# Two attention blocks: projections to queries and keys from parts, and a new order of work at both ends

## Time and profile before

| | us |
|---|---|
| three runs | 1654.03, 1655.61, 1656.54 |
| the profiled execution | 1653.08 |
| its span, first to last instruction | 1651.3 |
| head, until the first score of block 0 | 47.4 |
| round 0, round 1 | 80.9, 93.4 |
| a steady round | 97.0 |
| last round with scores (round 15) | 84.0 |
| from the last score of block 0 to the end | 83.5 |

### The profile page before, as it was taken

One profiled execution on the slowest core, in us unless ns is written; L12 is line 12 of the kernel. 1 busy time (PEld: TensorE's weight loads), 2 busy tenths in 40 slices (PEclk: granted clock), 3 DMA queues, 4 the chain that ended last, 5 costly groups with the idle time before them and its releaser, 6 DMA issues.

```text
span 1651.3 us, 25703 instructions
## 1 busy us (share of the span) xinstructions
PE 1598.8 (97%) x9399; PEld 1071.2 (65%) x9399; DVE 1159.9 (70%) x1961; ACT 1068.6 (65%) x1826; POOL 1120.6 (68%) x531
## 2 busy tenths in 40 slices
PE   7898999999999999999999999999999999999988
PEld 5333566666676766667676676766666666676667
DVE  6676676777767777776777777677777767766342
ACT  1454666766676666667666676766667676666744
POOL 2487767876766777676687767678676667868700
PEclk8899999999999999999999999999999999999999
DMA  7404032040412314141130414114041411400000
GB/s 208 122 20 121 20 97 52 33 126 29 128 39 81 68 33 116 39 129 39 68 80 33 116 39 128 34 58 96 21 128 39 124 31 39 109 20 8 7 7 20
DMA packets 47660, 111.69 MB, mean 68 GB/s; under 512 B 5808, under 2 KB 6448, under 8 KB 47536
## 3 DMA queue, kind: packets, MB, share of 16 engines
q1 hardware_dynamic: 47248, 109.86, 23.8%
q10 hardware_dynamic: 288, 0.20, 0.0%
HBM read 67.84 MB, written 41.94 MB: 66 GB/s over the span
## 4 chain that ended last, share of the span: by engine, by line
PE 89%; DVE 5%; ACT 3%; DMA 2%; issue 1%; SPq 0%; POOL 0%; ACTq 0%; POOLq 0%
PE bank L938 14%; PE acc L863 14%; PE scores L906 14%; PE scores L845 14%; PE scores L893 7%; PE bank L947 4%; PE scores L885 3%; PE acc L943 3%; DVE halfmax L724 3%; PE scores L886 3%; PE scores L887 3%; PE bank L943 3%; PE bank L969 2%; PE bank L965 2%; ACT turned L579 1%
## 5 line engine op out<-in xcount | busy, mean ns | idle before, releaser
L518 POOL TENSOR_TENSOR sum<-sum,probs 128x1024 f32<-128x1024 f32 x444 | 1040.1, 2373 | 372.1 <-PE acc L863 372.1
L724 DVE TENSOR_REDUCE halfmax<-bank 128x1 f32<-128x512 f32 x1007 | 666.8, 685 | 232.6 <-PE bank L938 228.9
L559 ACT ACTIVATE probs<-scores 128x512 f32<-128x512 f32 x896 | 515.9, 598 | 186.8 <-PE scores L845 183.2
L845 PE MATMUL scores<-q_stack,k_stack 97*128 97x512 f32 x1024 | 447.9, 454 | 2.4 <-DMA q_stack<-neg 2.3
L938 PE MATMUL bank<-k_stack,q_stack 96*128 96x512 f32 x992 | 422.7, 444 | 19.1 <-DVE halfmax L724 8.6
L938 PEld LDWEIGHTS bank<-k_stack,q_stack 96*128 96x128 f32 x992 | 187.0, 191 | 139.9 <-DVE halfmax L724 75.4
L906 PEld LDWEIGHTS scores<-v,turned 128*128 128x128 f32 x1952 | 252.3, 191 | 38.7 <-ACT turned L579 19.2
L906 PE MATMUL scores<-v,turned 128*128 128x128 f32 x1952 | 259.5, 276 | 4.3 <-ACT turned L579 3.8
L845 PEld LDWEIGHTS scores<-q_stack,k_stack 97*128 97x128 f32 x1024 | 194.2, 191 | 98.0 <-issue 79.6
L572 ACT ACTIVATE probs<-scores,negmax 128x1024 f32<-128x1024 f32 x128 | 142.6, 1114 | 157.9 <-DVE negmax L763 157.9
L863 PE MATMUL acc<-probs,v 128*32 128x512 f32 x1792 | 221.9, 607 | 0.0
(11 more groups left out here) (102 smaller groups left out, 1376.4 us busy)
## 6 DMA issues: line engine op xcount, KB each, us to landing
q_stack<-parts_dram SPq DMA_DIRECT2D x96, 256.0 KB, 5.2
k_stack<-parts_dram SPq DMA_DIRECT2D x96, 256.0 KB, 7.0
xin<-x_dram SPq DMA_DIRECT2D x16, 512.0 KB, 3.5
parts_dram<-q_hi SPq DMA_DIRECT2D x16, 512.0 KB, 2.6
parts_dram<-q_lo SPq DMA_DIRECT2D x16, 512.0 KB, 3.1
parts_dram<-k_hi SPq DMA_DIRECT2D x16, 512.0 KB, 3.7
parts_dram<-k_lo SPq DMA_DIRECT2D x16, 512.0 KB, 4.1
x<-x_dram SPq DMA_DIRECT2D x16, 512.0 KB, 3.5
```

What stands on the lines that cost most here:

```text
L518: pool.tensor_tensor(total, total, probs[:, ring_slot(i, half, kt), 2 * two:2 * two + 2, :], ALU.add).then_inc(added[two], 1)
L559: act.activation(dst, score_bank(i, index), ACT.Exp).then_inc(exp_done, 1)
L724: dve.tensor_reduce(halfmax[:, h, t, half:half + 1], banks[p][:, :], AX.X, ALU.max).then_inc(bank_free[p][VE], 1)
L845: pe.matmul(score_bank(i, index), ks[0:SPLIT + 1, i % 2, h, tile(kt)], qs[0:SPLIT + 1, q_half(i, half), h, :], start=True, stop=True).then ...
```

## The change

It does five things.

1. `q` and `k` of block 0 (images 1 to 15) and of block 1 (images 0 to 14) are projected in three fp32r products instead of one in fp32. The weights are split once at the start, the normalized image in each round: `hi0`/`hi1` on ScalarE write `xh_hi` by the same instruction as `norm`, `lo0`/`lo1` on VectorE subtract.
2. The tables are dealt anew: places of the maxima, `norm0`, `save`, `affine`, `scale`, `form` and `rstd`; `exp1` of even tiles one gap later.
3. The head: statistics of image 1 before the first maxima, from x1, where the image is loaded third; values at gaps 18 and 19; `q` and `k` in another order.
4. In round 0 and the last round with scores the first value product stands alone at gap 5 (`pv_a`); before, it was the first of the pair at gap 11.
5. The last two rounds have tables of their own (ROUND_END, new LAST_AT and chain).

```diff
 def tile_pieces(t, first):
-            ("exp1", t, 0, None, first + 1, None),
-            ("rinv", t, 0, None, None, first + 3),
+            ("exp1", t, 0, None, first + 2 - t % 2, None),
+            ("rinv", t, 0, None, None, first + 3 + 2 * (t % 2)),
...
 NEXT0 = [
-    ("affine0", 0, 2, None, None, 61), ("norm0", 0, 2, None, GAPS + 1, None),
+    ("affine0", 0, 2, None, None, 59),
+    ("norm0", 0, 2, None, GAPS + 0, None),
+    ("hi0", 0, 2, None, GAPS + 0, None),
+    ("lo0", 0, 2, None, None, GAPS + 3),
...
-    ("norm1", 0, 0, None, GAPS + 31, None), ("q1", 0, 0, GAPS + 36, GAPS + 36, GAPS + 37),
+    ("norm1", 0, 0, None, GAPS + 32, None),
+    ("hi1", 0, 0, None, GAPS + 32, None),
+    ("lo1", 0, 0, None, None, GAPS + 35),
+    ("q1", 0, 0, GAPS + 36, GAPS + 36, GAPS + 37),
...
 HEAD = [
-    ("norm0", 0, 0, None, 4, None),
-    ("q0", 0, 0, 5, 5, 6), ("q0", 1, 0, 5, 5, 6), ("k0", 0, 0, 7, 7, 8), ("k0", 1, 0, 7, 7, 8),
-    ("v0", 0, 0, 9, 9, None), ("v0", 1, 0, 9, 9, None),
+    ("norm0", 0, 0, None, 0, None), ("stats0", 0, 1, None, None, 0),
+    ("q0", 0, 0, 1, 1, 1), ("k0", 0, 0, 2, 2, 2), ("mean0", 0, 1, 3, None, 3), ("k0", 1, 0, 4, 4, 4),
+    ("q0", 1, 0, 5, 5, 5), ("var0", 0, 1, 6, None, 6),
 ] + [("max", n, 0, 10 + n, None, 10 + n) for n in range(FIRST)] + [
-    ("stats0", 0, 1, None, None, 20), ("mean0", 0, 1, 24, None, 24), ("var0", 0, 1, 28, None, 28),
-    ("affine0", 0, 1, None, None, 10 + FIRST),
+    ("v0", 0, 0, 18, 18, None), ("v0", 1, 0, 19, 19, None), ("affine0", 0, 1, None, None, 20),
...
-FIRST_MAX = [g for g in (*range(4), *range(10, 22)) for _ in range(2)]
+FIRST_MAX = [*range(4), *(g for g in range(10, 24) for _ in range(2))]
...
+    ("pv_a", 0, 0, 5, None, None), ("pv_b", 0, 0, 11, None, None)] + [
...
+def end_tile_pieces(t, offset, first):
+    return [("score1", (t, 0), offset, first, None, None), ("score1", (t, 1), offset, first + 1, None, None),
+            ("max1", t, offset, None, None, first + 1), ("exp1", t, offset, None, first + 1, None),
+            ("rinv", t, offset, None, None, first + 3), ("turn", t, offset, first + 4, first + 4, None),
+            ("pv1a", t, offset, first + 7, first + 7, None), ("pv1b", t, offset, first + 7, None, None)]
...
-LAST_AT = {tile: LAST_FIRST + LAST_SPACE * n for n, tile in enumerate(LAST_TILES)}
+LAST_AT = {tile: LAST_FIRST + LAST_SPACE * n + 3 * (tile[1] == -1) for n, tile in enumerate(LAST_TILES)}
...
+LAST_CHAIN = [
+    ("save", 1, -1, None, 4, None), ("sums", 1, -1, 4, 4, None), ("recip", (1, 0), -1, None, None, 5),
+    ("recip", (1, 1), -1, None, None, 5), ("recip", (1, 2), -1, None, None, 8), ("recip", (1, 3), -1, None, None, 8),
+    ("proj", 1, -1, 14, None, 14), ("stats1", 1, -1, None, None, 14),
+    ("mean1", 0, -1, 16, None, 15), ("var1", 0, -1, 17, None, 16), ("affine1", 0, -1, None, None, 17),
+    ("norm1", 0, -1, None, 18, None),
+    ("q1", 0, -1, 20, 20, 20), ("q1", 1, -1, 20, 20, 20), ("k1", 0, -1, 22, 22, 22), ("k1", 1, -1, 22, 22, 22),
...
+ROUND_LAST = LATER + [p for p in folded(VALUES) if p[2] == -1] + LAST_CHAIN + LAST_BLOCK1 + [
...
+NOT_IN_ACC = (("k0", 0, 0), ("q0", 0, 1), ("k0", 0, 1))
...
 @block.sync
             sp.dma_start(wts[:, :, :], weights).then_inc(const_loaded, 16)
+            sp.dma_start(x1[:, 1, :], x_dram[1]).then_inc(x1_loaded, 16)
...
-            for i in range(3):
+            load_shift(0, 0)
+            for i in (0, 2):
                 sp.dma_start(x1[:, i, :], x_dram[i]).then_inc(x1_loaded, 16)
-            load_shift(0, 0)
...
 @block.scalar
+            def high_norm(b, i):
+                before = parts_user_before(b, i)
+                if before:
+                    act.wait_ge(bank_full[bank_of(before)], filled(before))
+                act.wait_ge(affine_done[b], i + 1)
+                src = xin[:, :] if b == 0 else x1[:, i % 3, :]
+                act.activation(xh_hi[:, :], src, ACT.Identity, bias=gn[b][:, OFFSET:OFFSET + 1],
+                               scale=gn[b][:, GAIN:GAIN + 1]).then_inc(xh_high_done[b], 1)
...
+            act.wait_ge(prep_ve, 4)
+            for n in range(4):
+                act.copy(w_hi[:, n, :], weight_of(n)).then_inc(w_high_done, 1)
...
 @block.vector
+            def low_norm(b, i):
...
+                dve.wait_ge(norm_done[b], i + 1)
+                dve.wait_ge(xh_high_done[b], parts_before(b, i) + 1)
+                dve.tensor_tensor(xh_lo[:, :], xh[:, :], xh_hi[:, :].bitcast(F32),
+                                  ALU.subtract).then_inc(xh_low_done[b], 1)
...
+            for n in range(4):
+                dve.wait_ge(w_high_done, n + 1)
+                dve.tensor_tensor(w_lo[:, n, :], weight_of(n), w_hi[:, n, :].bitcast(F32),
+                                  ALU.subtract).then_inc(w_low_done, 1)
...
 @block.tensor
-                    pe.wait_ge(norm_done[b], i + 1)
-                    weight = wq_scaled[:, b, :] if name[0] == "q" else w(b, WK)
-                    mm = pe.matmul(dst[:, :], weight, xh[:, halves(arg)], start=True, stop=True)
+                    n = 2 * b + (name[0] == "k")
+                    if in_parts(b, i):
+                        pe.wait_ge(w_low_done, 4)
+                        pe.wait_ge(xh_low_done[b], parts_before(b, i) + 1)
+                        pe.matmul(dst[:, :], w_hi[:, n, :], xh_hi[:, halves(arg)], start=True, stop=False)
+                        pe.matmul(dst[:, :], w_hi[:, n, :], xh_lo[:, halves(arg)], start=False, stop=False)
+                        mm = pe.matmul(dst[:, :], w_lo[:, n, :], xh_hi[:, halves(arg)], start=False, stop=True)
+                    else:
+                        pe.wait_ge(norm_done[b], i + 1)
+                        mm = pe.matmul(dst[:, :], weight_of(n), xh[:, halves(arg)], start=True, stop=True)
```

More of the change, by code:

```diff
@@ L94 @@
 ]
 CHAIN = [
[L96 to L100, removed]
@@ new lines @@
+    ("sums", 0, 0, 45, 45, None),
+    ("recip", (0, 0), 0, None, None, 51),
+    ("recip", (0, 1), 0, None, None, 52),
+    ("recip", (0, 2), 0, None, None, 54),
+    ("recip", (0, 3), 0, None, None, 57),
+    ("proj", 0, 0, 60, None, 62),
+    ("stats1", 0, 0, None, None, 62),
+    ("save", 1, 0, None, GAPS + 3, None),
+    ("sums", 1, 0, GAPS + 7, GAPS + 7, None),
+    ("recip", (1, 0), 0, None, None, GAPS + 10),
+    ("recip", (1, 1), 0, None, None, GAPS + 11),
+    ("recip", (1, 2), 0, None, None, GAPS + 14),
@@ new lines @@
+END_AT = {(n % KT, n // KT - 2): TILE_FIRST + TILE_GAPS * n - GAPS for n in range(3, 3 + KT)}
+TILE_PIECES = ("score1", "max1", "exp1", "rinv", "turn", "pv1a", "pv1b")
+END_PIECES = [("out", 0, -2, 16, None, 16), ("pv_a", 0, 0, 5, None, None), ("pv_b", 0, 0, 11, None, None),
+              ("affine1", 0, -1, None, None, 30), ("norm1", 0, -1, None, 33, None)]
+ROUND_END = [p for p in ROUND if p[0] not in TILE_PIECES and p[:3] != ("pv", 0, 0)
+             and p[:3] not in [q[:3] for q in END_PIECES]] + END_PIECES
@@ L133 @@
+END_TILES = folded([p for (t, offset), first in END_AT.items() for p in end_tile_pieces(t, offset, first)])
 DIRECT = 2
@@ L181, in pieces_of @@
 def pieces_of(kind, i, engine, gap, images):
-    table = HEAD if kind == "head" else ROUND_FIRST if i == 0 else ROUND_LAST if i == images else ROUND
+    table = (HEAD if kind == "head" else ROUND_FIRST if i == 0 else ROUND_END if i == images - 1
+             else ROUND_LAST if i == images else ROUND)
     return [(p[0], p[1], i + p[2]) for p in table if p[engine] == gap and 0 <= i + p[2] < images]
@@ L212, in bank_uses @@
         if piece[0] in BANKED:
-            shared = (0, 1, 3, 4) if head_maximum(piece) else (0, 1)
-            b = 2 if piece[0] in IN_ACC and piece[1] == 0 else min(shared, key=lambda n: free[n])
+            shared = (0, 1, 3, 4) if in_head(piece) else (0, 1)
+            in_acc = piece[0] in IN_ACC and piece[1] == 0 and piece not in NOT_IN_ACC
+            b = 2 if in_acc else min(shared, key=lambda n: free[n])
             uses[piece] = (b, sum(counts[b]), counts[b][0], counts[b][1], last[b])
@@ L281, in bass_two_attention_blocks @@
         xh = sb("xh", [C, N])
+        xh_hi, xh_lo = (sb(n, [C, N], F32R) for n in ("xh_hi", "xh_lo"))
+        w_hi, w_lo = (sb(n, [C, 4, C], F32R) for n in ("w_hi", "w_lo"))
         part = [sb(n, [C, N], F32R) for n in ("q_hi", "q_lo", "k_hi", "k_lo")]
@@ L397, in turned_of, with hi_count, in_parts, parts_before @@
             return probs[:, 0, 2:4, :].rearrange("p h n -> p (h n)") if tile_set(j, t) else turned[:, :]
+        def hi_count(b, which, half, i):
+            order = ((0, 0), (1, 0), (1, 1), (0, 1)) if (b, i) == (0, 0) else ((0, 0), (0, 1), (1, 0), (1, 1))
+            return 4 * i + order.index((which, half)) + 1
+        def in_parts(b, i):
+            return i > 0 if b == 0 else i < images - 1
+        def parts_before(b, i):
+            return i - 1 if b == 0 else i
+        def parts_user_before(b, i):
+            if b == 0:
```

(6 more changed lines are left out.)

111 lines of the change are left out of this document (69 added, 42 removed).

## The result

The changed kernel takes 1761.29 us (median of 4 runs, 1760.03 to 1768.33) against 1655.63: a ratio of 1.0652, 95% interval [1.0635, 1.0669]. I had forecast 1632 us, faster.

What follows compares the result with a forecast made beforehand. TensorE, busy 97% of the span, was taken to bound the steady rounds. Terms of -17.3 - 1 + 4 - 4.5 - 1 - 4 = -23.8 us gave 1632 us; range 1616 to 1648 us, 8 times in 10.

Steps and rivals of the forecast that it cites:

- The shared reads of VectorE and GpSimd: At gaps 0 to 9: the two-SBUF-input subtraction might wait 0 to 2.35 us for GpSimd's addition, on average 1.2, twice a round.
- 4 us for all stalls that the parts bring: Steady rounds: splitting the image delays maxima and projections by 0.3 us a round over 14 rounds, +4 us.
- a rival of 0.07: Slower case, chance 0.07: each of 30 subtractions waits 1.2 us for GpSimd's addition and TensorE with it, 36 us; 1668 us.
- the rival's sign: Profile after: subtraction durations spreading up to 3.6 us beside GpSimd's additions would show the slower case at work.
- The projections: Queries and keys: three fp32r matmuls, 0.70 us, for one fp32 of 0.86; 108 in TensorE-bound rounds save 17.3 us.
- ScalarE's second pass: Writing xh_hi: one more ScalarE pass of 1.24 us per image and block, hidden in throughput by idle time.
- New places of the maxima: Steady rounds: 64 maxima dealt anew, within the 0.3 us a round charged for stalls; lower bound a gain of 1 us.
- The head: Before the first score: earlier first maximum 1.5, statistics moved 3.7, value projections costing 0.7; 4.5 us sooner, bounds 2 and 6.
- Rounds 0 and 1: GpSimd's first addition starts some 11 us sooner; 1 us gained in round 0, none in round 1; bounds +3 and -5 us.
- Tail and round 15: Last round before the tail and tail: copies 1 us, reordered work 2.5, last round 0.5; 4 us gained, bounds 0 and 8.
- The sum: Whole kernel: -17.3 - 1 + 4 - 4.5 - 1 - 4 = -23.8 us, forecast 1632 us, chance 0.51.

Runs made afterwards that it cites:

- e3: Changed kernel, with GpSimd made to wait before the addition that runs beside each subtraction until xh_lo is written; 1637.0 us, 0.9904 of the kernel before.
- e2: Changed kernel, with two bn_stats of one SBUF input on VectorE in place of each subtraction, xh_lo left zero; 1632.1 us, 0.9869 of the kernel before.
- e5: Kernel before, plus one unread VectorE subtraction with two SBUF inputs at gap 28 of every round; 1700.3 us in one run.
- e6: Kernel before, plus one unread VectorE subtraction in each of rounds 1 to 15, at gap 22 + i in round i; 1705.2 us in one run.
- e11: Kernel before, plus one unread VectorE subtraction in each of rounds 1 to 14, at gap 34 + 2i in round i; 1701.3 us in one run.
- e1: Changed kernel, with all query and key projections back to one fp32 matmul and no passes writing xh_hi and xh_lo; 1651.2 us, 0.998 of the kernel before.
- e7: Changed kernel with GpSimd's additions held for the subtraction, and image 0's values projected last in the head; 1630.6 us, 0.9849 of the kernel before.

## Why the prediction was wrong

The step that failed is "The shared reads of VectorE and GpSimd". I put the subtraction at 1.25 us into the sum, with 4 us for all stalls that the parts bring, and left the exclusion to a rival of 0.07. Where I had those 4 us, the exclusion alone measured 124 us (the changed kernel less e3) to 129 us (less e2). The mechanism of the rival is what happened, and I had it mis-sized twice. Its wait was to be what is left of one addition, 1.2 us on average; it was 3.5 us (4744 less 1226 ns), since 29 of 29 stood to the end of the row, and all 29 took longer than the 3.6 us that I had named as the rival's sign. And a stopped TensorE was to cost the stop alone; it cost the slow clock behind it too. For each of the 26 subtractions of the steady rounds that is 2.8 us of stop and 1.5 us of slow clock (72 and 39 us), where the rival had 1.2. So 1668 us became 1761. Against the case I had written that the wait "must reach TensorE through the maxima, under a pair of value products": for block 0 it did reach it, because behind the pair (553.80 to 555.7) only two maxima's matmuls, a score and `turn` were left before the next maximum needed a bank; for block 1 the projection one gap later had no cover that held, and TensorE waited for `xh_lo` itself. The rows that should have moved me were at hand: additions without a gap at both places where the subtraction was put. For block 0's place that is the earlier trace rows; for block 1's, about 761 us in that round, it is this row of the kernel before:

```profile
747.87 16.42 POOL L518 TENSOR_TENSOR sum<-sum,probs 128x1024 f32<-128x1024 f32 x7
```

The Trainium skill (SBUF — State Buffer, "Who interferes with whom") has the exclusion and the pairs of instructions it holds for; e2 and e3 agree with it. The same page ("Summary: rules for kernel authors") says that the second to come blocks until the first finishes. The traces go beyond: of 62 subtractions that met an addition with a further one behind it (changed kernel, e5, e6, e11), 39 had to let further additions pass.

Point by point, of the rest:

- *The projections.* Right. From e1 to e3, which differ in the parts and the hold alone, thirteen rounds fall by 15.3 us, 1.18 a round; 1.28 (8 x 0.16) less 0.3 was forecast. The triple's steps are 0.23 us.
- *ScalarE's second pass.* Right: 1.23 us, and without a stall that could be seen in e2 or e3.
- *New places of the maxima.* I charged 0.3 us a round for all stalls; by e1 the places alone gain 0.3.
- *The head.* Wrong. The first maximum came at 18.55 us, 2.4 us sooner, and the statistics were gone from between, but the two value projections took 2.0 us each at the low clock, instead of 1.16, and the four banks ran empty behind each: VectorE stood for 2.9 us twice, 5.8 us where I had counted 0.7. The clock of the head fell from 0.77 to 0.73. With the values out of the way e7 has 4.0 of the 4.5 us that I forecast.
- *Rounds 0 and 1.* Wrong in sign: round 0 lost 1.7 us (2.1 in e3), and round 1 2.5 in e3. What takes it is open; rounds 0 and 1 differ by up to 5 us between kernels that are the same there.
- *Tail and round 15.* The tail gained 5.6 us, and round 15 lost 3.0 in e1 to e3; I had 3.5 and 0.5 gained. Together 2.6 against 4.
- *The sum.* With e2, in which the exclusion is gone, 1632.1 us were measured where 1632 were forecast, and that is luck: head and rounds 0 and 1 lost 3.6 us where I had 6.5 gained (4.5, 1 and 1), and rounds 2 to 14 gained 21.0 us where I had some 13 (17.3 less 4).

Open: what decides whether a subtraction gets in behind the addition in progress or has to wait to the end of the row. The point within the addition (e6), the number of additions left (e11) and how long the data of the next one had been ready (4.0 to 9.2 us at the end of the one in progress where VectorE had to wait, 4.2 to 8.5 us where it got in) do not sort the cases. The 29 subtractions of the changed kernel all waited, and so show nothing of the choice.

## What to carry to other kernels

An instruction of VectorE with two inputs in SBUF is priced by what GpSimd does beside it, not by its columns: look for rows of GpSimd instructions without a gap at the place where it is put, and if there are any, let GpSimd wait for it by a semaphore, which here cost GpSimd 1.4 us a wait of idle time it had. A stop of TensorE is to be priced with the slow stretch that may follow: here 72 us of stops brought 39 us of slow clock. And before work is moved into a stretch, read the granted clock there: the value projection of 1.16 us took 2.0 us at the lower level.

## What the runs showed of the hardware

- A subtraction of 1024 fp32 columns from two SBUF tiles takes 1.22 us alone and up to 14.4 us beside GpSimd's additions, where bn_stats of one SBUF tile and maxima from PSUM keep their 0.68 us.
- Who waits is not fixed: when VectorE got in, the next addition took 3.3 us instead of 2.4; in the other cases up to six additions passed at full speed.
- With each of the 13 stops of 3.8 us in the steady rounds of the changed kernel the granted clock was 0.50 for 3 to 7 us, and TensorE's steps were 0.43 us instead of 0.23; with the 13 stops of 1.8 us it was so three times. In the same rounds of e3, without such stops, it stayed at 1.00.
